# Causal attention in a four-layer kernel: key tiles taken in pairs, four exponential buffers, and the inverse of the denominator on ScalarE and GpSimd

## The reference, cut to what matters

```
scores = einsum('bhqd,bhkd->bhqk', rope(q), rope(k)) / sqrt(32)
attn   = softmax(where(causal, scores, -inf), axis=-1)
out    = einsum('bhqk,bhkd->bqhd', attn, v).reshape(b, t, c) @ out_w.T + out_b
```

## Time and profile before

| what | value |
|---|---|
| runs (three) | 1527.41, 1529.63, 1530.99 us |
| median | 1529.63 us |
| span of the profiled execution | 1527.3 us |
| attention units 0 to 7, first score matmul to the end of the last `pv` | 905.9 to 1245.7 us of the span |
| PE busy over the span | 1465.1 us (96%) |
| DVE, ACT, POOL busy | 976.4, 614.1, 472.3 us |

### The profile page before, as it was taken

The page is one execution under the profiler, slowest core; times in us unless marked ns, Lnnn a source line. Parts: engine busy times, 40 slices in busy tenths (PEclk is TensorE's granted clock), DMA queues, the critical chain, the costliest instruction groups (busy, mean ns, idle before and its releaser), DMA issues. The chain is left out here.

```text
span 1527.3 us, 22410 instructions
## 1 busy us (share of the span) xinstructions
PE 1465.1 (96%) x7681; PEld 1072.6 (70%) x7696; DVE 976.4 (64%) x1897; ACT 614.1 (40%) x1079; POOL 472.3 (31%) x391
## 2 busy tenths in 40 slices
PE   7999989999999999999999999999999999999987
PEld 5788778788888888888888774444444458777554
DVE  6888987854545554454233666778787557667664
ACT  4343455613421441342121124555554546432544
POOL 1233334303420440241152231211223237103773
PEclk9999999999999999999999989999999999999999
DMA  6121347504320430334256685666556445853336
GB/s 215 34 71 65 152 166 248 180 14 138 96 69 29 151 96 27 110 96 149 82 191 192 207 244 138 192 198 155 155 173 213 150 152 218 303 208 132 105 101 238
DMA packets 105228, 223.38 MB, mean 146 GB/s; under 512 B 9328, under 2 KB 35312, under 8 KB 104240
## 3 DMA queue, kind: packets, MB, share of 16 engines
q1 hardware_dynamic: 101392, 211.96, 42.8%
q0 software_dynamic: 3744, 10.23, 2.2%
HBM read 157.54 MB, written 64.36 MB: 145 GB/s over the span
## 5 line engine op out<-in xcount | busy, mean ns | idle before, releaser
L2009 ACT ACTIVATE at_pt<-at_st 128x512 f32<-128x512 f32 (+3 forms) x384 | 164.1, 499 | 147.4 <-PE at_st L2039 146.5
L969 POOL TENSOR_TENSOR ff_w_lo<-ff_raw,ff_w_hi 128x1024 fp32r<-128x1024 f32 x64 | 153.7, 2402 | 220.8 <-ACT ff_w_hi L999 206.6
L115 PE MATMUL op_bank<-ff_x_hi,ff_w_lo 128*128 128x512 f32 x512 | 199.9, 390 | 0.2 <-issue 0.2
L116 PE MATMUL op_bank<-ff_x_lo,ff_w_hi 128*128 128x512 f32 x512 | 199.6, 390 | 0.0
L117 PE MATMUL op_bank<-ff_x_hi,ff_w_hi 128*128 128x512 f32 x512 | 199.5, 390 | 0.0
L1239 DVE TENSOR_TENSOR ff_h_lo<-ff_hf,ff_h_hi 128x512 f32 (+1 forms) x64 | 146.8, 2293 | 53.9 <-ACT ff_h_hi L1127 53.6
L999 ACT ACTIVATE ff_w_hi<-ff_raw 128x1024 fp32r<-128x1024 f32 x64 | 67.9, 1063 | 118.3 <-PE op_bank L117 116.0
L2039 PE MATMUL at_st<-mx_qp,mx_kp 98*128 98x512 f32 (+3 forms) x288 | 103.0, 390 | 12.6 <-ACT at_pt L2009 9.5
L1384 DVE CUSTOM_DVE_ANT_0 mx_mx<-mx_mx,mx_mask 128x128 f32<-128x128 f32 (+2 forms) x200 | 101.5, 517 | 21.1 <-PE mx_mx L1372 20.0
L115 PEld LDWEIGHTS op_bank<-ff_x_hi,ff_w_lo 128*128 128x128 f32 x512 | 96.4, 188 | 20.7 <-issue 0.6
L117 PEld LDWEIGHTS op_bank<-ff_x_hi,ff_w_hi 128*128 128x128 f32 x512 | 96.4, 188 | 20.4
(11 more groups left out here) (467 smaller groups left out, 3333.4 us busy)
## 6 DMA issues: line engine op xcount, KB each, us to landing
ff_raw<-in_Wug SPq DMA_DIRECT2D x64, 512.0 KB, 3.6
at_raw<-in_expert_gu SPq DMA_DIRECT2D x16, 704.0 KB, 12.1
mx_qp<-q_hi SPq DMA_DIRECT2D x12, 512.0 KB, 6.5
mx_kp<-k_hi SPq DMA_DIRECT2D x12, 512.0 KB, 11.6
at_raw<-in_expert_d SPq DMA_DIRECT2D x8, 768.0 KB, 13.7
expert_gu_bf<-at_cast SPq DMA_DIRECT2D x16, 352.0 KB, 10.9
ex_e_gu<-expert_gu_bf SPq DMA_DIRECT2D x8, 704.0 KB, 8.3
tm_ln_res<-in_x SPq DMA_DIRECT2D x4, 1024.0 KB, 5.5
```

Source lines behind the costliest of these rows:

```text
L115: pe.matmul(out, cut_l(ll), cut_r(rh), start=first, stop=False, **kw)
L116: pe.matmul(out, cut_l(lh), cut_r(rl), start=False, stop=False, **kw)
L969: pool.tensor_tensor(w[j][1][:, :, :, :], raw[:, j], f32(w[j][0][:, :, :, :]), ALU.subtract)\
L2009: act.activation(pt[:, s % PT, h, off:TB], st[(s * HG + h) % ST][:, off:TB], ACT.Exp, scale=SCALE).then_inc(exp_done, 1)
```

## The change

Steps are taken in pairs. PE does the scores of two steps and then `pv` of the two steps before; `pt` holds four steps. The pieces are spread anew: `FRONT` goes from 12 to 8, and steps 0 to 9 carry the others, so that every step carries four (in unit 0, steps 0 to 9 carry 48). When a `qc` has ended, ACT copies `den` and DVE copies `num`, each behind its work for the pair that follows. The reciprocal goes: ACT takes the logarithm of the denominator and the exponential of its negative (`near_inverse`, after the exponentials of step 7 for the first `qc` and of step 3 of the next unit for the second), and POOL does one Newton step and the product in four operations on 128x512 elements (`divide`: for the second `qc` of the unit before, at step 4 ahead of the casts; for the first, at step 10 ahead of that step's mask). The table set that ACT loads ahead of the attention is one with both functions, the set that the time-mix layer loads too. At the start ACT and DVE wait for the stores of the values, as SP did already.

```diff
-        act.preload_act_table(ACT.Exp)
+        act.preload_act_table_set("natural_log_exp_and_others")
...
-    LAST_PIECES, TURN_STEP, FRONT = 8, 9, 12
-    LAG = 2
-    PT = LAG + 1
+    PAIR = 2
+    TURN_STEP, FRONT = 9, 8
+    PT = 2 * PAIR
...
-            if s <= LAST_PIECES:
+            if s <= TURN_STEP:
                 begin = FRONT if u else 0
                 count = NP - begin
-                lo, hi = (begin + count * n // (LAST_PIECES + 1) for n in (s, s + 1))
+                lo, hi = (begin + count * n // (TURN_STEP + 1) for n in (s, s + 1))
...
+            def divide(u, qc):
+                n = u * QC + qc
+                pool.wait_ge(near_ready, 2 * n + 2)
+                pool.tensor_tensor(den_sb[:, qc, :], den_sb[:, qc, :], near[:, :], ALU.mult).then_inc(divided, 1)
+                pool.wait_ge(divided, n * DIVIDE_OPS + 1)
+                pool.tensor_scalar(den_sb[:, qc, :], den_sb[:, qc, :], -1.0, 2.0, ALU.mult, ALU.add).then_inc(divided, 1)
+                pool.tensor_tensor(num_sb[:, qc, :], num_sb[:, qc, :], near[:, :], ALU.mult).then_inc(divided, 1)
+                pool.wait_ge(divided, n * DIVIDE_OPS + 3)
+                pool.tensor_tensor(num_sb[:, qc, :], num_sb[:, qc, :], den_sb[:, qc, :], ALU.mult).then_inc(divided, 1)
...
+                    if u and s == TT:
+                        divide(u - 1, 1)
                     if s == TT:
                         for n in range(PER_UNIT):
                             narrow.narrow(pool, u * PER_UNIT + n)
...
+                    if s == TURN_STEP + 1:
+                        divide(u, 0)
...
+            divide(UNITS - 1, 1)
             expert_gpsimd(pool)
...
+            def near_inverse(u, qc):
+                n = u * QC + qc
+                act.wait_ge(copied, (n + 1) * 2)
+                at_least(act, divided, n * DIVIDE_OPS)
+                act.activation(near[:, :], den_sb[:, qc, :], ACT.Ln).then_inc(near_ready, 1)
+                act.wait_ge(near_ready, 2 * n + 1)
+                act.activation(near[:, :], near[:, :], ACT.Exp, scale=-1.0).then_inc(near_ready, 1)
...
-                at_least(act, pv_done, u * NS + s - LAG)
+                at_least(act, pv_done, u * NS + s - PT + 1)
...
+            for u, steps in pairs():
+                for s in steps:
+                    exps(u, s)
+                    if u and s == 2 * PAIR - 1:
+                        near_inverse(u - 1, 1)
+                    if s == 4 * PAIR - 1:
+                        near_inverse(u, 0)
+                    if u == UNITS - 1:
+                        for i, ks in SPLITS.get(s, ()):
+                            out.high(act, i, ks, pv_done)
+                ended = ended_before(u, steps)
+                if ended:
+                    copy_den(*ended)
...
+                for s in steps:
+                    scores(u, s)
+                if before:
+                    for s in before[1]:
+                        pv(before[0], s)
+                if TURN_STEP in steps and u + 1 < UNITS:
+                    mx.turn(pe, u + 1)
...
-            def invert(u, qc, chunk):
...
-                dve.reciprocal(den_sb[:, qc, cols], den_sb[:, qc, cols]).then_inc(inverted, 1)
...
+            def copy_num(u, qc):
+                dve.wait_ge(pv_done, u * NS + ENDS[qc] + 1)
+                at_least(dve, o_stored[qc], u * DMA)
+                dve.tensor_copy(num_sb[:, qc, :], num[:, :]).then_inc(copied, 1)
```

More of the change, by code:

```diff
@@ L1922, in pieces_at, with pairs, ended_before @@
             return [(u + 2, n) for n in range(lo, hi)]
-        def place(g):
-            return g // NS, g % NS
+        def pairs():
+            return [(u, [s, s + 1]) for u in range(UNITS) for s in range(0, NS, PAIR)]
+        def ended_before(u, steps):
+            s = steps[0] - 1
+            if s in ENDS:
+                return u, ENDS.index(s)
+            return (u - 1, QC - 1) if s < 0 and u else None
         @block.sync
@@ L1996, in _, with copy_den @@
         def _(act):
-            def copy_out(u, qc):
+            def copy_den(u, qc):
                 act.wait_ge(pv_done, u * NS + ENDS[qc] + 1)
@@ L2010, in exps @@
                                    scale=SCALE).then_inc(exp_done, 1)
[L2012 to L2018, removed]
+            for stored in mx.v_stored:
+                act.wait_ge(stored, NB * TT // 2 * DMA)
+            for u, steps in pairs():
[12 more added lines that the diff above has]
+                if TURN_STEP in steps and u + 1 < UNITS:
                     mx.negate_high(act, u + 1)
[L2020 to L2023, removed]
+            copy_den(UNITS - 1, QC - 1)
+            near_inverse(UNITS - 1, 1)
             out.high(act, 2, range(KT), pv_done)
@@ L2062, in _ @@
             pe.wait_ge(ones_small_set, 1)
-            for g in range(UNITS * NS):
-                u, s = place(g)
-                if s == 0:
+            before = None
+            for u, steps in pairs():
+                if steps[0] == 0:
                     pe.wait_ge(mx.ones_set, min(u + 1, SLOTS))
                     pe.wait_ge(mx.rows_loaded, (u + 1) * 2 * DMA)
[L2068 to L2071, removed]
+                for s in steps:
[3 more added lines that the diff above has]
+                        pv(before[0], s)
+                if TURN_STEP in steps and u + 1 < UNITS:
                     mx.turn(pe, u + 1)
-            for g in range(UNITS * NS - LAG, UNITS * NS):
-                pv(*place(g))
+                before = u, steps
+            for s in before[1]:
+                pv(before[0], s)
             for i in range(NB - 1):
@@ L2089, in _ @@
[L2089 to L2093, removed]
+            def copy_num(u, qc):
+                dve.wait_ge(pv_done, u * NS + ENDS[qc] + 1)
+                at_least(dve, o_stored[qc], u * DMA)
+                dve.tensor_copy(num_sb[:, qc, :], num[:, :]).then_inc(copied, 1)
+            for u, steps in pairs():
+                if u == 0 and steps[0] == PAIR:
+                    for stored in mx.v_stored:
+                        dve.wait_ge(stored, NB * TT // 2 * DMA)
+                for s in steps:
+                    for of, n in pieces_at(u, s):
+                        mx.top(dve, of, n)
+                    if u == UNITS - 1:
+                        if s == OW_STEP:
+                            ow.low(dve)
+                        for i, ks in SPLITS.get(s, ()):
+                            out.low(dve, i, ks)
+                if TURN_STEP in steps and u + 1 < UNITS:
@@ L2094, in _ @@
                     mx.join(dve, u + 1)
-                if s == TURN_STEP and u + 1 < UNITS:
+                ended = ended_before(u, steps)
+                if ended:
+                    copy_num(*ended)
+                if TURN_STEP in steps and u + 1 < UNITS:
                     mx.negate_low(dve, u + 1)
[L2097 to L2107, removed]
+            copy_num(UNITS - 1, QC - 1)
             out.add(dve, 0)
```

21 lines of the change are left out of this document (7 added, 14 removed).

## The result

The changed kernel takes 1509.8 us (median of four runs, 1507.98 to 1511.68) where the kernel before took 1529.7: a ratio of 0.9872, with a 95% interval from 0.9858 to 0.9885. The forecast was 1509. The profiled execution has a span of 1508.7 us (its own device time was 1510.53) against 1527.3 before. The number was met more closely than its terms, and that is luck: units 1 to 5 gained less than forecast and unit 7 lost more, while two falls of the clock that went, and a start that came 1.9 earlier, were in no term and made up for it.

What follows compares the result with a forecast made beforehand. Scores were taken as held up by DVE's queue, ACT's copies and cold starts, pv by columns plus 0.14 per change. Terms 18.25 + 3.5 + 0.95 - 0.95 - 1.4 = 20.35 gave 1509 us, range 1504 to 1514.

Steps and rivals of the forecast that it cites:

- The pv term: pv stretches in each unit: six changes instead of twelve, at 0.14 each, taken as 0.75 us less per unit.
- The pairs: Six score pairs per unit, each at the later of two chains: sum 22.35 instead of 25.26, 2.9 us less.
- rival F: PE, ACT and DVE in lockstep, each pair 0.5 longer, 3 per unit: no change, 1530; chance 0.07.
- Step 6: Scores before the change: 2.90 against step 5's 2.02, blamed on two ACT copies of 0.60 ahead of the exponentials.
- The two falls "where they are": Clock falls behind step 10 of units 1 and 5, pv 3.38 instead of 1.86, assumed to stay.
- Rival C: More gained: pairs of 3.6 on average and both clock falls gone, 1.5 each: 1501; chance 0.12.
- Unit 7: Last unit: splits between a pair's exponentials lose 2.4, against gains of 0.75 and 0.7; net loss 0.95.
- Division and masks: POOL's division at 4.95, bounds 2.6 and 6.0, hidden ahead of masks 10 and 11 with 1 to 1.7 spare.
- rival B: POOL late for masks 10 and 11: division of 8, PE waits 1.5 per unit, 1519; chance 0.10.
- Rival A: DVE's tops locked out while POOL divides, at steps 4, 5 and the next unit's first pair: slower, 1545; chance 0.09.
- Tail: Behind the last pv: division on POOL delays the bias addition and second projection; loss 1.4, bounds 0 and 2.8.
- Rival D: ACT's table set loads at each change of function: about 10 more, 1519; chance 0.02.

Runs made afterwards that it cites:

- E6: Changed kernel without the inverse: logarithm, exponential and GpSimd's four operations left out, numerator stored undivided; 1509.0 us.
- E1: Kernel before with only the inverse moved to ScalarE and GpSimd, steps still one by one, pieces as before; 1523.3 us, ratio 0.9966.
- E3: Changed kernel with the old spread of pieces, twelve with steps 10 and 11; 1529.4 us, ratio 1.0008.
- the repeat: Changed kernel run once more unaltered, for a second profile; 1503.7 us.
- E5: Changed kernel with seven more GpSimd operations of 0.62 ahead of each division of the first qc; 1532.7 us, ratio 1.0022.
- E7: E4 plus the last division on DVE straight from PSUM, so that POOL adds the bias at once; 1505.7 us, ratio 0.9846.
- E2: Changed kernel with reciprocals and product back on DVE at the steps where they stood before; 1552.4 us, ratio 1.0154.
- E4: Changed kernel with the last unit's splits behind the exponentials of both steps of a pair; 1505.4 us, ratio 0.9851.
- the repeat of E4: E4 run once more unaltered, for a second profile; 1507.0 us.

## Why the prediction was right, and where it wasn't

In a unit without a fall the mechanism held: 3.15 of the 3.65 forecast came, from the shorter scores and the fewer changes to `pv`, and the inverse cost nothing there (E6). Term by term:

- *The pv term* (0.75, fixed cost 0.14 a change): 0.82 measured; right.
- *The pairs* (22.35): 22.81, and 22.93 with the turn; mis-sized by 0.5. The later of two chains was taken for each pair. Three of the six pairs came out 0.14 to 0.19 longer: 4.05, 4.09 and 3.64, the last with the turn's 0.12 in it. The timeline of the fourth pair, steps 6 and 7 (PE, PEld and DVE), shows why for that one:

```profile
1049.18 0.14 DVE L1384 DVE_READ_ACCUMULATOR2_ANT mx_tops<- 128x1 f32 x1
...
1049.38 0.19 PEld L1372 LDWEIGHTS mx_mx<-mx_kp,mx_qp 96*128 96x128 f32 x1 [0.33 <-DVE mx_tops L1384]
...
1049.66 0.40 PE L2076 MATMUL at_st<-mx_qp,mx_kp 98*128 98x512 f32 x1
```

The last score could go at about 1049.3, when the fifth exponential ended (ACT has four in 2.10 us from 1048.18 on, and it is the second of them); but a piece stands ahead of it that waits for a top until 1049.38. That is rival F's mechanism, some 0.3 in this pair. F priced it at 0.5 in each pair, and the six came out 0.1 longer on average.
- *Step 6* was read as ACT's: its two copies ahead of the exponentials. E1 leaves both copies and still takes 0.48 of the 0.88 by which step 6 was longer than step 5, so that DVE's reciprocal and product had the larger half. (In the item below it "0.60" is when the first exponential begins; its bank is free at its end, about 0.6 later, as the sum for the eighth score has it.)
- *The two falls "where they are"* was the step that failed: they went in both profiles of the changed kernel, worth 3.0 here. Rival C had named that, and priced it right, but tied it to shorter pairs, which didn't come. E3 shows what took them away: with twelve pieces in the pair of steps 10 and 11 six falls come in units 0 to 5. The twelve pieces alone don't explain it, since E1 has them too, in two separate stretches of 2.35 to 2.77, and no fall in units 1 to 5.
- *Unit 7*: the splits cost 2.35 where 2.4 was forecast; the fall in that unit (2.70, in the repeat 1.70) was in no term, and since the kernel before fell there in one of its two profiles (40.39 instead of 37.22), part of the 4.2 is the choice of the execution.
- *Division and masks*: 4.60 measured (4.95 forecast). In unit 3 of the changed kernel POOL had:

```profile
1064.62 1.28 POOL L1988 TENSOR_TENSOR at_den_sb<-at_den_sb,at_near 128x512 f32<-128x512 f32 x1
1065.99 0.62 POOL L1990 TENSOR_SCALAR at_den_sb<-at_den_sb 128x512 f32<-128x512 f32 x1
1066.57 1.29 POOL L1991 TENSOR_TENSOR at_num_sb<-at_num_sb,at_near 128x512 f32<-128x512 f32 x1
1067.94 1.29 POOL L1993 TENSOR_TENSOR at_num_sb<-at_num_sb,at_den_sb 128x512 f32<-128x512 f32 x1
1069.18 1.22 POOL L2012 TENSOR_SCALAR_AFFINE_SELECT at_pt<-at_pt 128x512 f32<-128x512 f32 x2
```

Masks 10 and 11 ended at 1070.40, their `pv` began at 1071.92: rival B had 1.5 us to go, as forecast (1 to 1.7), and E5 shows the wait behind them.
- *Rival A* fell: the longest of the 112 reductions over 512 columns in the attention took 0.693, before and after, and without any division (E6) the unit is no shorter. The Trainium skill's rule (SBUF — State Buffer, "Who interferes with whom") had it so for operations with one input in SBUF. It also has the converse, and the trace shows it where DVE's splits, with two inputs there, met POOL's division in unit 7:

```profile
1216.61 2.44 DVE L1817 TENSOR_TENSOR at_o_lo<-at_raw_o,at_o_hi 128x512 fp32r<-128x512 f32 x2 [1.19 <-ACT at_o_hi L1811]
```
```profile
1216.79 1.71 POOL L1988 TENSOR_TENSOR at_den_sb<-at_den_sb,at_near 128x512 f32<-128x512 f32 x1
1218.59 0.94 POOL L1990 TENSOR_SCALAR at_den_sb<-at_den_sb 128x512 f32<-128x512 f32 x1
```

1.71 and 0.94 instead of 1.28 and 0.62, and 2.44 for two splits that take 1.4 alone; nothing waited for them.
- *Unit 0* (-3.5 forecast, -2.9 measured) can't be told from one execution: the changed kernel took 46.22 and, in the repeat, 43.17.
- *Tail*: the first addition waited for the bias, and the second projection for it, 1.2 later against the last `pv` than before:

```profile
1237.05 0.69 DVE L195 TENSOR_TENSOR at_ln_res<-mx_mx,at_ln_res 128x512 f32<-128x512 f32 x1 [10.66 <-POOL at_ln_res L1825]
1237.80 0.50 PE L115 MATMUL mx_mx<-ow_w_hi,at_o_lo 128*128 128x512 f32 x1 [1.04 <-DVE at_ln_res L195]
```

The first matmul of the layer of experts began 40.0 behind the last `pv` (40.1 in the repeat), where it had begun 38.7 behind it in both profiles of the kernel before; with the division out of the bias's way it is 38.7 again (E6, E7). So the mechanism is right, with 1.3 for 1.4; the row before and the row in the changed kernel:

```profile
1284.41 1.04 PE L2605 MATMUL at_st<-ex_ident,ex_turned_in 128*128 128x128 f32 x8
```
```profile
1265.60 1.03 PE L2643 MATMUL at_st<-ex_ident,ex_turned_in 128*128 128x128 f32 x8
```

The length to the end of the span is too unsteady to show it: 281.6 and 281.1 before, 283.2 and 280.2 in the changed kernel. That the table's +1.6 is so near is in part luck.

- *Rival D* fell: ACT loads no table within the attention.

What stays open: what sets a fall off. Long starved stretches make it likely (E2, E3), but half of the falls there come a few stretches later, E4's unit 7 had none where three profiles of the same code had one, and E7's profile had two behind steps 10 and 11 (3.6 long, in units 4 and 5) that E4's, with the same code there, had not:

```profile
1105.79:1110.62 4.83, 4.83 (x34) 1.21 (x33) 0.83 (x3) 0.01 (x1) 4.66 (x5) 0.65 0.00 0
```

## What to carry to other kernels

Price a long starved stretch of matmuls with what comes behind it: here a score stretch that was almost 2 us longer (E2, E3) cost up to 2.7 more in the next `pv` or up to 1.7 in a later one, and spreading the same work evenly gained twice (E3). Where two chains feed one in-order queue in turns, add something to the later of them; here it was a tenth of a microsecond on average. Work moved to a third engine is free as long as what is queued behind it there has time, and that time is set by the slowest thing ahead of it, here a DMA.

## What was not expected of the hardware

The granted clock falls behind stretches in which PE waits much: here directly behind scores of 4.98 (the changed kernel), 5.43 (E2) and 5.91 us (E3), but also behind scores of 4.47 (E2), 3.94 (E3) and 3.6 (E7), while 5.19 (E2) and 5.47 (E3) were followed by a `pv` at full clock. The stretch that pays ran mostly at 0.50 (E5) to 0.72 (the repeat of E4). The same kernel shows it in other places and with other lengths in another execution. Unit 0 took 46.22 us in one profile of the changed kernel, where its first scores ran at 0.50, and 43.17 in the other, where they ran at 1.00; with unit 7 (41.46 and 40.17) that makes 4.3 of the 6.8 us between their spans (1508.7 and 1501.9).
